# Attention's output products from float32r parts of the sums and of the weights, in three passes of 130 columns, in place of float32 products of 129

## The reference

```
Q = (x @ Wq.T).reshape(b, n, H, R)      # H = 8 heads, R = 64
K = (x @ Wk.T).reshape(b, n, H, R)
V = (x @ Wv.T).reshape(b, n, H, d)      # d = 128
attn = softmax(einsum('bnhr,bmhr->bhnm', Q, K))
out = einsum('bhnm,bmhd->bnd', attn, V)
x = x + ga * out
```

## Time and profile before

| | us |
|---|---|
| median of 3 runs | 2828.07 |
| lowest and highest of them | 2826.57, 2828.36 |
| the profiled execution, its own time | 2826.37 |
| its span in the trace | 2824.6 |
| PE busy in the span | 2669.2 |
| PE weight loads busy | 2040.7 |
| DVE, ACT, POOL busy | 2206.3, 2209.9, 1917.8 |

### The profile page before, as it was taken

One profiled execution on the slowest core, in us unless ns is written; L12 is line 12 of the kernel. 1 busy time (PEld: TensorE's weight loads), 2 busy tenths in 40 slices (PEclk: granted clock), 3 DMA queues, 4 the chain that ended last, 5 costly groups with the idle time before them and its releaser, 6 DMA issues. The chain is left out here.

```text
span 2824.6 us, 78341 instructions
## 1 busy us (share of the span) xinstructions
PE 2669.2 (94%) x27878; PEld 2040.7 (72%) x27878; DVE 2206.3 (78%) x8368; ACT 2209.9 (78%) x4485; POOL 1917.8 (68%) x2020
## 2 busy tenths in 40 slices
PE   5999999999999999999999999789999999999788
PEld 3777777877777777777777778566666666666644
DVE  6567876776776776876876865699999999999676
ACT  3888888888888888888888887368878878878566
POOL 3788888888888888887888878325455455455134
PEclk7999999999999999999999999778878878878799
DMA  3000000000000000000000100200000000000000
GB/s 111 1 1 1 9 1 1 9 1 1 8 1 1 8 1 1 8 1 1 8 1 1 42 1 9 102 1 0 0 0 0 0 0 0 0 0 0 2 23 38
DMA packets 12272, 27.88 MB, mean 10 GB/s; under 512 B 1592, under 2 KB 6200, under 8 KB 11840
## 3 DMA queue, kind: packets, MB, share of 16 engines
q1 hardware_dynamic: 12096, 25.74, 2.6%
HBM read 17.33 MB, written 8.40 MB: 9 GB/s over the span
## 5 line engine op out<-in xcount | busy, mean ns | idle before, releaser
L316 POOL TENSOR_TENSOR probs_l<-probs,probs_h 128x512 fp32r<-128x512 f32 x1024 | 1304.3, 1298 | 285.8 <-ACT probs_h L411 280.9
L410 ACT ACTIVATE probs<-bank 128x512 f32<-128x512 f32 x1024 | 640.3, 625 | 259.4 <-PE bank L766 163.6
L600 DVE TENSOR_REDUCE maxes<-ring 128x1 f32<-128x512 f32 x1024 | 659.5, 686 | 185.4 <-PE ring L746 185.1
L411 ACT ACTIVATE probs_h<-bank 128x512 fp32r<-128x512 f32 x1024 | 641.8, 627 | 0.0
L765 PE MATMUL bank<-q_hh,k_hl 128*128 128x512 f32 x1024 | 424.5, 415 | 1.3 <-ACT probs_h L411 1.1
L766 PE MATMUL bank<-q_lm,k_h 65*128 65x512 f32 x1024 | 405.5, 396 | 0.0
L776 PE MATMUL obank<-probs_h,x_l 128*128 128x512 f32 x1024 | 404.4, 395 | 0.0
L778 PE MATMUL obank<-probs_h,x_h 128*128 128x512 f32 x1024 | 403.4, 394 | 0.0
L777 PE MATMUL obank<-probs_l,x_h 128*128 128x512 f32 x1024 | 402.7, 393 | 0.0
L746 PE MATMUL ring<-k_hl,q_hh 128*128 128x512 f32 x1024 | 336.7, 410 | 7.9 <-DVE k_hl L583 3.9
L1187 ACT ACTIVATE low_hot<-obank 128x512 f16<-128x512 f32 x512 | 297.1, 604 | 55.2 <-PE obank L1432 42.1
(11 more groups left out here) (282 smaller groups left out, 4932.2 us busy)
## 6 DMA issues: line engine op xcount, KB each, us to landing
xt<-in_x SPq DMA_DIRECT2D x8, 512.0 KB, 7.8
x<-out_x SPq DMA_DIRECT2D x1, 4096.0 KB, 12.6
out_x<-x SPq DMA_DIRECT2D x16, 256.0 KB, 2.0
out_x<-xt SPq DMA_DIRECT2D x7, 512.0 KB, 2.6
mod<-out_x SPq DMA_DIRECT2D x3, 512.0 KB, 15.2
spare<-in_w_q SPq DMA_DIRECT2D x2, 512.0 KB, 5.7
spare<-in_w_qT SPq DMA_DIRECT2D x2, 512.0 KB, 7.0
hot_rule<-in_hot_rule SPq DMA_DIRECT2D x1, 1024.0 KB, 7.7
```

The costliest lines, as they stand in the source:

```text
L316: nc.gpsimd.tensor_tensor(probs_l[:, i, :], probs[:, s % 4, :], probs_h[:, i, :].bitcast(F32), ALU.subtract).then_inc(low_ready, 1)
L410: nc.scalar.activation(probs[:, s % 4, :], st[s % 4], ACT.Exp)
L411: nc.scalar.activation(probs_h[:, i, :], st[s % 4], ACT.Exp).then_inc(st_free[s % 4], 1)
L600: nc.vector.tensor_reduce(maxes[:, i, k:k + 1], ring[bank_of(at)][:], AX.X, ALU.max).then_inc(rows_maxed, 1)
```

## The change

The weights and the sums are each kept as two float32r tiles, a high part (the value rounded to float32r) and a low part (what is left). ACT writes the high part where it wrote the float32 tile. DVE takes the low parts with a subtraction that reads the same PSUM bank: `fine_weights` 128x128, once a head, and `fine_sums` 128x512, twice a head. The four float32 products of `outputs` become twelve float32r ones: high sums by low weights, high by high, low sums by high weights. The width goes from 129 to 130 columns, the last of zeros. `w_ready` and `sum_read` are now counted up by DVE, after ACT's new `w_h_ready` and `sum_h_ready`.

```diff
-        w_out = [sb(f"w_out{i}", [P, D + 1]) for i in range(2)]
-        sums = [sb(f"sums{i}", [P, HALF]) for i in range(2)]
+        w_out_h = [sb(f"w_out_h{i}", [P, D + 2], F32R) for i in range(2)]
+        w_out_l = [sb(f"w_out_l{i}", [P, D + 2], F32R) for i in range(2)]
+        sums_h = [sb(f"sums_h{i}", [P, HALF], F32R) for i in range(2)]
+        sums_l = sb("sums_l", [P, HALF], F32R)
...
-                nc.scalar.activation(w_out[h % 2][:, 0:D], ring[bank_of(at)][:, 0:D], ACT.Copy).then_inc(w_ready, 1)
+                nc.scalar.activation(w_out_h[h % 2][:, 0:D], ring[bank_of(at)][:, 0:D], ACT.Copy).then_inc(w_h_ready, 1)
...
-                nc.scalar.activation(sums[half][:], obank[half][:], ACT.Copy).then_inc(sum_read, 1)
+                nc.scalar.activation(sums_h[half][:], obank[half][:], ACT.Copy).then_inc(sum_h_ready, 1)
...
+            def fine_weights(b, h):
+                dve.wait_ge(w_h_ready, b * H + h + 1)
+                bank = ring[bank_of(located(b, "w", h))]
+                nc.vector.tensor_tensor(w_out_l[h % 2][:, 0:D], bank[:, 0:D], w_out_h[h % 2][:, 0:D].bitcast(F32), ALU.subtract).then_inc(w_ready, 1)
+
+            def fine_sums(b, h, half):
+                g = b * H + h
+                dve.wait_ge(sum_h_ready, 2 * g + half + 1)
+                if 2 * g + half:
+                    dve.wait_ge(o_full, 2 * g + half)
+                nc.vector.tensor_tensor(sums_l[:], obank[half][:], sums_h[half][:].bitcast(F32), ALU.subtract).then_inc(sum_read, 1)
...
+                        if s == 6 and g:
+                            fine_sums(b - (h == 0), (h - 1) % H, 1)
+                        if s == WEIGHTS:
+                            if more:
+                                fine_weights(b, h + 1)
+                            fine_sums(b, h, 0)
...
             for half in range(2):
+                if half:
+                    fine_sums(B - 1, H - 1, 1)
                 gather_output(link, B - 1, H - 1, half)
...
-                    out = bank[:, 0:D + 1] if j == 3 else obank[half][:, j * (D + 1):(j + 1) * (D + 1)]
-                    mm = nc.tensor.matmul(out, sums[half][:, j * P:(j + 1) * P], w_out[h % 2][:], start=True, stop=True)
+                    out = bank[:, 0:D + 2] if j == 3 else obank[half][:, j * (D + 2):(j + 1) * (D + 2)]
+                    four = slice(j * P, (j + 1) * P)
+                    nc.tensor.matmul(out, sums_h[half][:, four], w_out_l[h % 2][:], start=True, stop=False)
+                    nc.tensor.matmul(out, sums_h[half][:, four], w_out_h[h % 2][:], start=False, stop=False)
+                    mm = nc.tensor.matmul(out, sums_l[:, four], w_out_h[h % 2][:], start=False, stop=True)
```

More of the change, by code:

```diff
@@ L153, in build_attention @@
         product_done = sem("product_done")
+        sum_h_ready = sem("sum_h_ready")
         sum_read = sem("sum_read")
+        w_h_ready = sem("w_h_ready")
         o_full = sem("o_full")
@@ L613, in gather_output @@
                 one, t0 = ring[bank_of(at)], 4 * half
-                three = obank[half][:, 0:3 * (D + 1)].rearrange("p (j d) -> p j d", j=3)
+                three = obank[half][:, 0:3 * (D + 2)].rearrange("p (j d) -> p j d", j=3)
                 def add(t, o):
@@ L671, in _ @@
             dve.wait_ge(w_loaded, 48)
-            for t in w_out:
-                nc.vector.tensor_copy(t[:, D:D + 1], ident[:, P - 1:P]).then_inc(w_split, 1)
+            for t, l in zip(w_out_h, w_out_l):
+                nc.vector.tensor_copy(t[:, D:D + 1], ident[:, P - 1:P])
+                nc.vector.tensor_scalar(t[:, D + 1:D + 2], ident[:, P - 1:P], 0.0, None, ALU.mult)
+                nc.vector.tensor_scalar(l[:, D:D + 2], ident[:, P - 2:P], 0.0, None, ALU.mult).then_inc(w_split, 1)
             for n in range(3, 5):
@@ L689, in _ @@
                 gated_values(0, part)
+            fine_weights(0, 0)
             whole_max(0, 0)
```

## The result

The changed kernel took 2912.45 us (2910.68 to 2913.91, four runs) against 2828.07; the ratio is 1.0298, with a 95% interval of 1.0286 to 1.0311. It is slower by 84 us, or 3%. Forecast were 2924, with a range of 2878 to 2965.

A forecast was written before the change was run, and what follows sets the result against it. PE was taken to bound the kernel, with its output products paced by 128-column weight loads. The terms 57 + 12 - 5 + 6 + 24 + 2 = 96 us on 2828 gave 2924 us, range 2878 to 2965.

The forecast's parts named there:

- What bounds: Attention stretch, 160 to 1760 us: PE is busy 1595 of 1600 us, so each microsecond on PE counts in full.
- item 1: PE's output products: twelve weight loads 0.112 us apart, 1.34 us a group in place of 0.90, +57 us.
- item 2: DVE's `fine_sums` at step 6: step 8's score product 0.19 us late per head, +12; step 5's wait goes, -5 us.
- item 3: DVE's low part of the weights at step 13 makes PE 0.1 us late at `turn_max`, 63 times, +6 us.
- item 4: DVE's half 0 low sums at step 13 delay norms; PE waits 3.5 us a batch at outputs, +24 us.
- item 5: The last `fine_sums` behind DVE's variance at the attention's end, with the set-up at the start, +2 us.
- Rival A: PE's loads pace the products but DVE's delays (items 2 to 4) vanish: 2887 us, chance 0.20.
- B: Columns pace the output products at 0.061 us each: 2846 us (0.05) or 2809, faster (0.03); chance 0.08.
- C: Each added DVE instruction makes PE wait its whole length, 96 us in all: 2981 us, chance 0.09.
- D: The 130-column float32r products run as float32 ones, two records each, +229 us: 3096 us, chance 0.03.

The follow-up runs named there:

- e6: The changed kernel with the low part of half 1's sums taken in two 256-column subtractions, after steps 6 and 7, in place of one: 2896.30 us.
- e2: The kernel before, float32 products kept, plus DVE's three low-part instructions a head and their waits; nobody reads the low parts: 2851.31 us.
- e3: The changed kernel with its output products 66 columns wide in place of 130, with loads, waits and DVE's work kept: 2910.97 us.
- e7: The changed kernel without the pass of high sums by low weights and without the low part of the weights: 2843.75 us.
- e12: The kernel before, with DVE waiting at step 13 for ACT's exponentials of step 14, so the norms start 2.7 us later: 2872.79 us (one run).

## Why the prediction was right

The sum was 96 us, measured were 84, and the mechanism that carried it holds: 57 of the 96 were PE's loads, and 58 came. The rest is less good than 84 beside 96 makes it look. The sum was for the attention, and there 79.4 us came; the other 5 lie behind it, where the forecast said that nothing changes, and helped the number by luck. Of the 39 us forecast for DVE's share (items 2 to 5) about 20 came.

- *What bounds.* PE is full before and after, and each 0.45 us put on it came out: right.
- *What paces the products* (item 1, +57): right, and the term that decided the sign. The load of 128 columns costs 0.111 to 0.112 us whether 8, 66 or 130 columns follow and whether the stationary block is new or the same. Steps 2 and 9 grew by 0.45 and 0.46: 64 x 0.91 = 58 us. The four passes that FP8 and Floating Point Precision (the Trainium skill, section TensorE Precision Notes) counts for true float32 are neither shown nor refuted by a run here, but the columns that follow from them don't give the price: by these, 390 in place of 516 would be faster; the change came out slower, and 66-column products no faster. Nor were the 81 ns seen that TensorE: Matmul & The Clock Gate (the Trainium skill, section Back-to-back issue gap) gives for pairs of load and product at 128 columns: the pairs are 111 to 112 ns apart.
- *Step 6's low part* (item 2, +12 and -5): the wait at step 8 is 0.17 where 0.19 was forecast. Less the 0.25 us that went in the first head of a batch, which the forecast did not have, that is about 9 us over all heads, and `e6` shows its cause. The 5 us to be won at step 5 did not come: that step is 1.72 us in both traces. I had taken DVE's lateness as the cause of the wait there, but in the changed kernel DVE itself waits for PE ahead of step 4's maxima, and the load's wait behind them is the same (0.25 us in the earlier trace rows):

```profile
839.92 1.29 DVE L616 TENSOR_REDUCE maxes<-ring 128x1 f32<-128x512 f32 x2 [0.43 <-PE ring L773]
...
841.26 0.19 PEld L773 LDWEIGHTS ring<-k_hl,q_hh 128*128 128x128 f32 x1 [0.26 <-DVE maxes L616]
```

- *The weights* (item 3, +6): step 14 grew by 0.05 and not 0.1, some 3 us. I missed who else uses that bank: in head 6 the transposes of the next batch, at step 13, wait 0.33 us seven times (2 us).
- *The sums of half 0 and the norms* (item 4, +24): this is the term that was mis-sized. The shift by 2.7 us was right (`w_out_h` ready, then 0.29 and 0.60), but PE waits (0.59 - 0.45) + (0.90 - 0.45) = 0.59 us a batch in place of 3.5, so 4 us in all. I took the norms' lengths as fixed; each lost 0.7 to 0.8 us, as one POOL subtraction fewer stood in their way. After head 4 nothing is late at all, and after head 0 the variance instruction took 0.17 us in place of 2.71.
- *The end* (item 5, +2): from the last score product to the attention's end it is 1.9 us longer, and 0.9 of these are the last two groups of item 1. With 0.3 at the start, 1.3 came.

In the attention that makes 58 + 9 + 3 + 2 + 4 + 1 = 77 of the 79.4 seen; the other 2 are spread over the other steps, some 0.01 or 0.02 us in each. Rival A (DVE's delays vanish, 2887) is the nearest miss, but DVE's share is real: `e2` took 23 us with it alone. B (the columns pace) is excluded by `e3` and `e7`, C (each added instruction exposed, 96 us) by `e2`, and D (two records a product) by the twelve records a group.

## What to carry to other kernels

Price a narrow matmul (130 columns and fewer here) by its weight load and not by its columns. Splitting one float32 product, which loads twice, into three float32r passes adds a load. It could pay where the moving side is wide enough to cover the loads; no run here tests that. A product of 8 columns somewhere in the same trace shows the floor. When PE gets faster, look for the engine that frees its banks: of the 57 us that one pass should have won, 22 came and 24 were held up by DVE at step 5; moving the score rows and DVE's additions to steps with room brought 13 more.

## What the runs showed of the hardware

Not expected: the norms' DVE instruction with its 128x128 operands in SBUF, 0.33 us by itself, takes up to 1.45 us when it meets a POOL subtraction, and ends 0.08 us behind that one. The low-part subtraction, which reads PSUM, kept its 0.68 us throughout (680 to 694 ns over 128, of which 127 overlap a POOL subtraction). SBUF — State Buffer (the Trainium skill, section SBUF: two separate sides) has it that VectorE, with some kinds of instruction, and GpSimd share a port pair as an exclusive lock for a whole instruction. The traces agree, in that the long ones end with POOL's instruction and not later; which ports are used no run shows. The length of such work depends on when it starts: 42 long ones of 128 became 28 by starting 2.7 us later (`e12`).
